# Quantizing the FFN weights inside the SSM stage through a DRAM spill, in place of a staging pass between the two stages

## What is computed

```
x = layernorm(x + ssm(x))        # stage A
x = layernorm(x + ffn(x))        # stage B

ssm:  u, gate = split(x @ W_in.T)             # 1024 -> 2 x 1024
      b = u @ W_state.T;  dt = min(softplus(u @ W_dt.T + b_dt), 10)
      decay = exp(-dt * rate)                  # 128 states
      h[t] = decay[t]*h[t-1] + (1-decay[t])*b[t]
      z = (h @ W_C.T) * silu(gate) + x*D;  out = z @ W_out.T

ffn:  h = relu(fq(fq(x, 8, 4) @ fq(w1, 8, 6).T + fq(b1, 8, 6), 8, 4))     # 1024 -> 4096
      out = fq(h, 8, 4) @ fq(w2, 8, 6).T + fq(b2, 8, 6)                   # 4096 -> 1024
fq(v, width, frac) = clip(round(v * 2**frac), -2**(width-1), 2**(width-1)-1) / 2**frac
```

## Time and profile before

| what | value |
|---|---|
| median of the runs shown | 3329.84 us |
| profiled execution, its own time | 3328.71 us |
| span of its slowest core (first to last instruction) | 3327.2 us |
| TensorE busy (matmuls) | 2864.5 us, 86% of the span |
| VectorE busy | 1974.9 us, 59% |
| ScalarE busy | 466.7 us, 14% |
| bytes moved by transfers | 128.10 MB |

### The profile page before, as it was taken

The page is one execution under the profiler, slowest core; times in us unless marked ns, Lnnn a source line. Parts: engine busy times, 40 slices in busy tenths (PEclk is TensorE's granted clock), DMA queues, the critical chain, the costliest instruction groups (busy, mean ns, idle before and its releaser), DMA issues.

```text
span 3327.2 us, 55273 instructions; the slowest of 8 cores (3316.5 to 3327.2 us)
## 1 busy us (share of the span) xinstructions
PE 2864.5 (86%) x21120; PEld 2094.4 (63%) x21120; DVE 1974.9 (59%) x5582; ACT 466.7 (14%) x979; POOL 19.0 (1%) x26
## 2 busy tenths in 40 slices
PE   2999999999206998999998999998998998998998
PEld 1444444444005777777777777777777777777776
DVE  0343443443586667777567776667777667777655
ACT  0323222322001111001111001111100111100100
POOL 0000000000000000000000000000000000000000
PEclk9999999999557999999999999999999999999999
DMA  9123332330570000000000000000000000000000
GB/s 124 26 39 38 51 46 31 51 51 23 170 250 26 20 20 26 20 20 33 21 20 27 20 20 32 21 20 26 20 20 22 30 20 26 20 20 20 27 14 26
DMA packets 109811, 128.10 MB, mean 39 GB/s; under 512 B 3936, under 2 KB 102240, under 8 KB 108528
## 3 DMA queue, kind: packets, MB, share of 16 engines
q1 hardware_dynamic: 71936, 83.89, 7.7%
q0 software_dynamic: 20976, 23.89, 6.2%
q10 hardware_dynamic: 16640, 16.78, 2.4%
HBM read 98.07 MB, written 50.33 MB: 45 GB/s over the span
## 4 chain that ended last, share of the span: by engine, by line
PE 74%; DVE 18%; issue 3%; DMA 2%; another core or an unknown queue 2%; DVEq 1%; ACT 0%; ACTq 0%; SPq 0%
PE pb L221 65%; PE pb L218 7%; DVE htmp8b L743 3%; DVE x_sb L605 2%; DVE htmp8b L750 2%; DVE hq_sb L758 2%; DVE htmp8b L685 2%; DVE x_sb L601 2%; DVE xq_sb L692 2%; DMA wstage_a<-w1T 1%; PE pb L554 1%; PE pb L559 1%; DMA wstage_a<-w2T 1%; DVEq L171 0%
## 5 line engine op out<-in xcount | busy, mean ns | idle before, releaser
L221 PE MATMUL pb<-xq_sb,w1q 128*128 128x256 bf16 x7168 | 955.5, 282 | 118.3 <-DVE row L521 112.2
L221 PE MATMUL pb<-hq_sb,w2q 128*128 128x256 bf16 x7936 | 934.5, 279 | 77.7 <-DVE hq_sb L758 77.7
L221 PEld LDWEIGHTS pb<-hq_sb,w2q 128*128 128x128 bf16 x7936 | 790.1, 100 | 203.0 <-issue 96.1
L221 PEld LDWEIGHTS pb<-xq_sb,w1q 128*128 128x128 bf16 x7168 | 715.4, 101 | 250.7 <-issue 143.3
L221 PE MATMUL pb<-xb,winT_sb 128*128 128x512 bf16 x1792 | 430.9, 381 | 64.0 <-DMA xb<-xT 60.7
L627 DVE SCALAR_TENSOR_TENSOR r_sb<-pb,b2q,x_sb 128x256 bf16<-128x256 f32 x256 | 123.3, 482 | 585.1 <-PE pb L218 585.0
L743 DVE TENSOR_SCALAR htmp8b<-pb,b1q 128x256 f32<-128x256 f32 x1024 | 425.1, 476 | 43.8 <-DVE hq_sb L758 30.9
L221 PEld LDWEIGHTS pb<-xb,winT_sb 128*128 128x128 bf16 x1792 | 174.8, 98 | 277.7 <-issue 71.4
L218 PE MATMUL pb<-xq_sb,w1q 128*128 128x256 bf16 x1024 | 288.4, 282 | 0.0
L758 DVE TENSOR_SCALAR hq_sb<-htmp8b 128x256 bf16<-128x256 f32 x1024 | 230.6, 289 | 28.2 <-DVE htmp8b L750 0.9
L750 DVE TENSOR_SCALAR htmp8b<-htmp8b 128x256 f32<-128x256 f32 x1024 | 230.6, 289 | 28.1 <-DVE htmp8b L743 0.9
(11 more groups left out here) (95 smaller groups left out, 1811.9 us busy)
## 6 DMA issues: line engine op xcount, KB each, us to landing
outT<-ob SPq DMA_DIRECT2D x32, 1024.0 KB, 4.5
xb<-xT POOLq DMA_DIRECT2D x16, 1024.0 KB, 17.5
r1s<-r_sb ACTq DMA_DIRECT2D x16, 1024.0 KB, 9.6
r1ld<-r1s SPq DMA_DIRECT2D x32, 512.0 KB, 4.1
wstage_a<-w1T SPq DMA_DIRECT2D x4, 2048.0 KB, 8.9
wstage_b<-w1T SPq DMA_DIRECT2D x4, 2048.0 KB, 9.5
wstage_a<-w2T SPq DMA_DIRECT2D x4, 2048.0 KB, 8.8
wstage_b<-w2T SPq DMA_DIRECT2D x4, 2048.0 KB, 8.7
```

The costliest lines, as they stand in the source:

```text
L221: E.matmul(o, l, r, **kw))
```

## The change

The staging pass between the stages goes. Each weight is instead quantized in 128x512 pieces, 64 of w1 and 64 of w2, eight pieces behind the `z_sb` sums of each of the 16 blocks of stage A. Four f32 staging buffers and four bf16 buffers lie on addresses that only stage B uses (`sqb1`, `sqb2`, `htmp8b`). SP loads a piece (256 KB), VectorE makes the same three passes on it, SP stores the bf16 result (128 KB) to a DRAM tensor (`w1qs`, `w2qs`). The first four loads are issued before the first block, behind the first three `xb` loads in program order but on SP's queue; the load of piece i+4 is issued when piece i has been quantized, behind the store of piece i. After `endA` and the last store, POOL reloads `w1q` and SP reloads `w2q` (8.4 MB each) from these tensors, SP loads the first two `r1ld` blocks behind, and TensorE waits for all of it.

```diff
+    w1qs = nc.dram_tensor("w1qs", [128, DC, HID], BF16, kind="Internal").ap()
+    w2qs = nc.dram_tensor("w2qs", [128, HC, D], BF16, kind="Internal").ap()
...
+    wstg = [sb("wstg_%d" % i, [128, 512], F32, "A",
+               at=handles["sqb1" if i < 2 else "sqb2"][1] + (i % 2) * 2048)
+            for i in range(4)]
+    woutq = [sb("woutq_%d" % i, [128, 512], BF16, "A",
+                at=handles["htmp8b"][1] + i * 1024) for i in range(4)]
...
+        def wq_issue(n):
+            for _ in range(n):
+                i = wqs["issued"]
...
+                si = i % 4
+                srcap, _, _ = wq_stages[i]
+                pre = []
+                if i >= 4:
+                    pre.append(("vd", wqs["vv"][i - 4]))
+                wqs["qv"].append(dma("Y", "qt%d" % si, wstg[si][:, :], srcap,
+                                     pre=pre))
+
+        def wq_quant(n):
+            for _ in range(n):
+                i = wqs["done"]
...
+                wait("V", "qt%d" % si, wqs["qv"][i])
+                if i >= 4:
+                    wait("V", "qws%d" % si, wqs["oq"][i - 4])
+                s = wstg[si][:, :]
+                v = op("V", lambda E, s=s: E.tensor_scalar(
+                    out=s, in0=s, scalar1=64.0, scalar2=MAGIC,
+                    op0=ALU.mult, op1=ALU.add), inc="vd")
+                wait("V", "vd", v, selfdep=True)
+                v = op("V", lambda E, s=s: E.tensor_scalar(
+                    out=s, in0=s, scalar1=MAGIC, scalar2=127.0,
+                    op0=ALU.subtract, op1=ALU.min), inc="vd")
+                wait("V", "vd", v, selfdep=True)
+                v = op("V", lambda E, s=s, o=woutq[si][:, :], pm=pm:
+                       E.tensor_scalar(out=o, in0=s, scalar1=-128.0, scalar2=pm,
+                                       op0=ALU.max, op1=ALU.mult), inc="vd")
+                wqs["vv"].append(v)
+                wqs["oq"].append(dma("Y", "qws%d" % si, dstap, woutq[si][:, :],
+                                     pre=[("vd", v)]))
+
+        wq_issue(4)
...
                 z_done[t] = vv
+                for _wq in range(8):
+                    wq_quant(1)
+                    wq_issue(1)
...
-        for k in range(DC):
-            stage_quant(w1q[:, k, :],
-                        w1T.rearrange("(k p) h -> p k h", p=128)[:, k, :],
-                        HID, k % 2)
-        for k4 in range(HC // 4):
-            stage_quant(w2q[:, 4 * k4:4 * k4 + 4, :],
-                        w2T.rearrange("(k p) e -> p k e", p=128)[:, 4 * k4:4 * k4 + 4, :],
-                        HID, k4 % 2, shape4=True, postmul=16.0 / 1024.0)
-        wq_done = wq_loads[-1][1]
+        spill_done = [("qws%d" % i, cnt["qws%d" % i]) for i in range(4)]
+        w1_rl = dma("G", "qwr", w1q[:, :, :], w1qs[:, :, :],
+                    pre=endA + spill_done)
+        w2_rl = dma("Y", "qw2r", w2q[:, :, :], w2qs[:, :, :],
+                    pre=endA + spill_done)
...
-                wait("T", "vd", wq_done)
+                wait("T", "qwr", w1_rl)
+                wait("T", "qw2r", w2_rl)
```

More of the change, by code:

```diff
@@ L152, in build_nc @@
             "qw", "qx0", "qx1", "qx2", "qa0", "qa1", "qy0", "qy1", "qo",
-            "qt0", "qt1", "qd", "tm", "sd", "vd")}
+            "qt0", "qt1", "qt2", "qt3", "qws0", "qws1", "qws2", "qws3",
+            "qwr", "qw2r", "qd", "tm", "sd", "vd")}
         prog = {e: [] for e in ENGS}
@@ L302, in build_nc @@
         load_xb(2)
+        w1rr = w1T.rearrange("(k p) h -> p k h", p=128)
+        w2rr = w2T.rearrange("(k p) e -> p k e", p=128)
+        wq_stages = []
+        for k in range(DC):
+            for c0 in range(0, HID, 512):
+                wq_stages.append((w1rr[:, k, c0:c0 + 512],
+                                  w1qs[:, k, c0:c0 + 512], 1.0 / 1024.0))
+        for k in range(HC):
+            for c0 in range(0, D, 512):
+                wq_stages.append((w2rr[:, k, c0:c0 + 512],
+                                  w2qs[:, k, c0:c0 + 512], 16.0 / 1024.0))
@@ new lines, in build_nc @@
+        wqs = {"issued": 0, "done": 0, "qv": [], "vv": [], "oq": []}
+        def wq_issue(n):
+            for _ in range(n):
+                i = wqs["issued"]
+                if i >= len(wq_stages):
+                    return
+                wqs["issued"] += 1
+                si = i % 4
[5 more added lines that the diff above has]
+                                     pre=pre))
@@ new lines, in wq_quant @@
+        def wq_quant(n):
+            for _ in range(n):
+                i = wqs["done"]
+                if i >= min(wqs["issued"], len(wq_stages)):
+                    return
+                wqs["done"] += 1
+                si = i % 4
+                _, dstap, pm = wq_stages[i]
+                wait("V", "qt%d" % si, wqs["qv"][i])
[16 more added lines that the diff above has]
+                                     pre=[("vd", v)]))
@@ L440, in build_nc @@
                     dbgA_qs[0] = cnt["qd"]
+        while wqs["done"] < len(wq_stages):
+            wq_quant(1)
+            wq_issue(1)
         endA = [("tm", cnt["tm"]), ("vd", cnt["vd"]), ("sd", cnt["sd"]),
                 ("qa0", cnt["qa0"]), ("qa1", cnt["qa1"])]
[L446 to L472, removed]
@@ L493, in load_r1 @@
             if tb < 3:
-                pre += endA + [("vd", wq_loads[-1][1])]
+                pre += endA
             if tb >= 2:
@@ L501, in build_nc @@
         load_r1(1)
-        prev_htmp_v = [wq_loads[-1][1]]
+        for _i in range(4):
+            wait("V", "qws%d" % _i, cnt["qws%d" % _i])
+        prev_htmp_v = [cnt["vd"]]
         prev_htmp_s = [0]
```

## The result

The changed kernel takes 3252.83 us (median of 9 runs) against 3330.29 (32 runs): ratio 0.9775, 95% interval 0.9762 to 0.9787, which is 75 us. The forecast was 3262 in a range of 3235 to 3296. Executions in which the cores of one die show a lower granted clock are left out of every comparison of times, so the run without `xb` loads, which has no others, is read by its waits alone, and the run with the reordered reload is shown by core 1, on its undisturbed die.

The account below looks back on a forecast made before the run. TensorE was taken as the bound, idle only in the hole between the stages. 3328.7 - 86.4 (hole) + 3.2 (start) + 15.6 (stage A stalls) = 3261.1, forecast 3262 us, range 3235 to 3296.

Parts of the forecast that it names:

- The hole: Between the stages: 17.3 MB at 320 GB/s plus 2.3 us, new hole 56.4 us, saving 86.4 us.
- The third rival: Reload between the stages: POOL's queue is slow, 166 GB/s, the hole is 84 us; 3289 us, chance 0.06.
- The start: Before TensorE's first matmul: four loads run beside POOL's weights and add 3.2 us (bounds 0 and 5.0).
- Stage A: Loads of pieces 4 to 7 land late beside `xb`; TensorE stalls 1.2 us in 13 blocks, 15.6 us.
- the prediction's own sign: Stage A, blocks 1 to 13: wait before the gate's fifth group names `c_t`; wrong if absent or over 3 us.
- The first rival: Stage A: all pieces hide, SP's packets served ahead of `xb`'s or filling its gaps; 3245.5 us, chance 0.30.
- The slack of 13.05 + 1.2 us: Stage A: VectorE's free time before `ld_t` plus a little more; up to 14.25 us after `z_sb` TensorE notices nothing.
- the prediction's estimate of 2.6 us: Stage A: the skill's fit, 2.0 us plus bytes at 436 GB/s, for a 256 KB load; no piece waits.
- the second rival: Stage A: loads' packets cost 156 ns, stall 3.4 us plus 1.7 for slow restart, 13 times; 3312 us, chance 0.12.
- The fourth rival: Stage A: SP's queue works off stores and loads one by one, TensorE stalls 112 us; 3357 us, chance 0.06.

Follow-up runs that it names:

- all three edits: Changed kernel with reload ordered `r1ld`, `w1q`, `w2q`, first piece loads after the first `xb` block, and eight buffers: 3194.3 to 3196.5 us, ratio 0.9606.

## Why the prediction was right, and where it was not

**The hole** went as worked out: 55.8 us on core 0 from the reload's issue, forecast 56.4. 17.3 MB at 320 GB/s plus 2.3 us was the term; with the same 2.3 us taken off, the measured rate is 17.3 / 53.5 = 323 GB/s, and 324 from the two landings above. The 320 was picked between two rows, 287 and 370; that it hit to 1% is luck, the bounds of 49 to 63 us were what the rows gave. The Trainium skill (HBM Reference, Specifications (TRN2)) gives about 358 GB/s a core when a pair streams. Counted as here, 17.3 MB to TensorE's start, no core of the changed kernel reached it (322 to 331 GB/s); in shorter stretches cores do come to it and above, 370 GB/s over 5 us in the earlier trace rows and 324 to 373 between the two landings of the reordered reload on cores 0 to 3. The third rival is out: the reload through POOL's queue landed 2 us behind the one through SP's (53.1 and 51.1 us), and with both on SP the second lands 57.7 us after the first one's issue.

**The start** was +3.2, and +3.4 came out. The cause is borne out by the mean starts of the two kernels with late loads (63.0 and 61.3), not by their times.

**Stage A** was the step that failed, in its size: "I take 1.2 us, nearer the slowest engine: 13 x 1.2 = 15.6 us". Measured is 1.0 us over the whole stage; TensorE waits for `c_t` 0 to 1.9 us in total, depending on the core. By the prediction's own sign ("wrong if that wait is absent") this part is wrong: the wait is absent on four cores and comes once on each of the others, and blocks 0, 14 and 15, which were to show no waits, show them. The first rival's result, 3245.5, is nearer to the measured time than the forecast's, which came within some 9 us because the hole, nearly all of the change, was right. The rival's mechanism is half right: the pieces hide, but not because nothing waits. On core 0 they wait in every block, with or without `xb`, because a load takes as long to come back as the three pieces ahead of it. The working that added the slowest engine's `xb` remainder to the four pairs described a queue that isn't the limit: without `xb` the waits remain, and with more loads in flight they vanish. The slack of 13.05 + 1.2 us was right to 0.15 us, as the 160 stalls with ten and sixteen pieces show, and it is what makes the waits cheap.

The loads took 4.2 us in the median, and 5.3 with eight in flight (core 0). The Trainium skill (DMA: Bandwidth & Descriptors, Anatomy of one DMA) states the fit behind the prediction's estimate of 2.6 us, and states it for transfers issued from GpSimd's queue. These loads are issued from SP's, so it isn't a fit for them. By 2.6 us no piece would have waited; the outcome for the time was almost the same, the reason was not.

**The slow restart** of the second rival is real, but the changed kernel doesn't show it: after each of its four stalls the first seven matmuls took the usual 1.67 us. After 12 to 14 us of idle time they took 3.15 us, after 3.25 us in one case the usual 1.67, while the earlier trace rows shows a slow restart after 2.12 us; what decides in between was not tried. The fourth rival (each pair of transfers in turn, the last piece ending 20 us after the sums) did not occur: the pieces end at most 14.2 us after the sums on core 0 and 16.3 on any core.

**Stage B** took 2.8 us more in the mean. It was forecast at 0, the cores scatter from 2314 to 2325 us over both kernels, and no experiment touched it. At half of the products with `w2q` the two kernels are level (1208.6 and 1208.8 us into the stage), so it arises long after the reload, and six other kernels with the reload show means of 2319.5 to 2321.0 too; why is left open.

## What to carry to other kernels

A pass that waits for transfers can be hidden in an idle stretch of an engine that isn't the bound; before moving it, read from the timeline at which instruction the bounding engine first notices (here a PSUM bank, 14.4 us on), and count the waits of the moved work into that budget as well as its busy time. The number of transfers in flight must cover the time to landing: four buffers against 4.2 us left waits that the slack still held with eight pieces and that cost 34 us with ten, and ten buffers gave those back. When a hole is filled with bytes in a line, look which of them the next instruction needs: ordering the reload by first use gave some 50 us more (49.7 in the hole with all three edits), over half of what the change itself had gained.

## What the runs showed that was not expected

Loads of 256 KB landed no sooner without the `xb` loads beside them than with them (medians of 4.4 to 4.8 against 4.2 to 4.5 us on four cores); why is open. With eight in flight the time to landing rose from 4.2 to 5.3 us on core 0, and every wait was gone all the same; in the kernel with all three edits, also with eight, it is 4.0 to 5.8 us by core. And the slack is sharp: a microsecond of VectorE past 14.4 us behind the sums was a microsecond of TensorE, to 0.01 us, in all 160 stalls.
